# Spectral weights copied by ScalarE into mode-wise rows, mixed sums stored by GpSimd, part of the weights loaded among images

## The reference, cut to what matters

```python
def spectral_conv2d(x, w1, w2):                       # MODES = 16
    x_ft = jnp.fft.rfft2(x)
    out_ft = out_ft.at[:, :, :MODES, :MODES].set(jnp.einsum('bixy,ioxy->boxy', x_ft[:, :, :MODES, :MODES], w1))
    out_ft = out_ft.at[:, :, -MODES:, :MODES].set(jnp.einsum('bixy,ioxy->boxy', x_ft[:, :, -MODES:, :MODES], w2))
    return jnp.fft.irfft2(out_ft, s=(h, w))
...
x1 = spectral_conv2d(x, w1, w2)                       # x: group-normed input, 16 x 64 x 128 x 128, fp32
x2 = jnp.einsum('bchw,oc->bohw', x, conv_w) + conv_b[None, :, None, None]
y_flat = (x1 + x2).transpose(0, 2, 3, 1).reshape(-1, c)
y_flat = kan_linear(y_flat, k1_base, k1_spline, k1_scaler, grid)   # silu and cubic splines, 64 x 64
y_flat = kan_linear(y_flat, k2_base, k2_spline, k2_scaler, grid)
return x + gelu(y)
```

## Time and profile before

| | us |
|---|---|
| median of 3 runs | 3696.25 |
| lowest and highest | 3695.16, 3698.87 |
| the profiled execution | 3700.55 |
| its span | 3698.7 |
| TensorE busy in it | 3629.4 (98%) |
| VectorE, ScalarE busy | 3480.8, 3374.5 |
| barrier to mix block | 248.72 |
| first inverse matmul of the second half | 334.23 |

### The profile page before, as it was taken

The page is one execution under the profiler, slowest core; times in us unless marked ns, Lnnn a source line. Parts: engine busy times, 40 slices in busy tenths (PEclk is TensorE's granted clock), DMA queues, the critical chain, the costliest instruction groups (busy, mean ns, idle before and its releaser), DMA issues.

```text
span 3698.7 us, 98607 instructions
## 1 busy us (share of the span) xinstructions
PE 3629.4 (98%) x36932; PEld 1565.2 (42%) x36932; DVE 3480.8 (94%) x3548; ACT 3374.5 (91%) x3510; POOL 116.3 (3%) x140
## 2 busy tenths in 40 slices
PE   8987999999999999999999999999999999999998
PEld 4555657654333333333333333333333333333333
DVE  8875999999999999999999999999999999999997
ACT  4433999999999999999999999999999999999997
POOL 0000000000000000000000000000000000000000
PEclk9998999999999999999999999999999999999999
DMA  9998243432322323223232232322323222232231
GB/s 320 328 214 200 61 120 89 118 93 60 76 69 65 77 58 76 68 66 77 58 76 67 67 74 60 77 66 68 73 61 77 64 70 71 63 77 64 70 73 50
DMA packets 269760, 338.45 MB, mean 92 GB/s; under 512 B 83272, under 2 KB 198824, under 8 KB 267624
## 3 DMA queue, kind: packets, MB, share of 16 engines
q1 hardware_dynamic: 248392, 265.50, 25.3%
q0 software_dynamic: 18720, 67.49, 10.1%
q10 hardware_dynamic: 2560, 4.20, 0.4%
HBM read 248.50 MB, written 88.61 MB: 91 GB/s over the span
## 4 chain that ended last, share of the span: by engine, by line
PE 90%; SPq 1%; issue 1%; DMA 1%; ACTq 0%; ACT 0%; DVE 0%; DVEq 0%
PE l_ps L1241 84%; PE y_banks L1218 3%; PE y_banks L1227 2%; SPq L160 1%; PE y_banks L1260 1%; PE y_banks L1202 1%; PE y_banks L1189 0%; PE y_banks L1241 0%; DMA big<-in_spec_w_i_dram 0%; ACTq L729 0%; ACT mixed L726 0%; DMA rows_scratch<-rows 0%; PE l_ps L1260 0%; DMA modes_scratch<-mixed 0%; PE mix_ps L705 0%
## 5 line engine op out<-in xcount | busy, mean ns | idle before, releaser
L1121 ACT ACTIVATE offset<-size 128x1024 f32<-128x1024 f32 x1280 | 1241.0, 1045 | 8.1
L1047 DVE SCALAR_TENSOR_TENSOR cube0r<-below,offset 128x1024 f32<-128x1024 f32 x256 | 312.6, 1221 | 113.2 <-ACT offset L1121 103.2
L1047 DVE SCALAR_TENSOR_TENSOR cube2r<-below,offset 128x1024 f32<-128x1024 f32 x256 | 311.5, 1217 | 0.6 <-PE l_ps L1241 0.6
L1047 DVE SCALAR_TENSOR_TENSOR cube0l<-above,offset 128x1024 f32<-128x1024 f32 x256 | 311.7, 1217 | 0.0
L1047 DVE SCALAR_TENSOR_TENSOR cube1r<-below,offset 128x1024 f32<-128x1024 f32 x256 | 311.6, 1217 | 0.0
L1047 DVE SCALAR_TENSOR_TENSOR cube1l<-above,offset 128x1024 f32<-128x1024 f32 x256 | 311.6, 1217 | 0.0
L1047 DVE SCALAR_TENSOR_TENSOR cube3r<-below,offset 128x1024 f32<-128x1024 f32 x256 | 311.5, 1217 | 0.0
L1047 DVE SCALAR_TENSOR_TENSOR cube2l<-above,offset 128x1024 f32<-128x1024 f32 x256 | 311.5, 1217 | 0.0
L1047 DVE SCALAR_TENSOR_TENSOR cube3l<-above,offset 128x1024 f32<-128x1024 f32 x256 | 311.5, 1217 | 0.0
L1047 DVE SCALAR_TENSOR_TENSOR cube4l<-above,offset 128x1024 f32<-128x1024 f32 x256 | 311.4, 1217 | 0.0
L1047 DVE SCALAR_TENSOR_TENSOR cube4r<-below,offset 128x1024 f32<-128x1024 f32 x256 | 311.4, 1216 | 0.0
(11 more groups left out here) (169 smaller groups left out, 5963.3 us busy)
## 6 DMA issues: line engine op xcount, KB each, us to landing
big<-in_x_dram SPq DMA_DIRECT2D x128, 512.0 KB, 8.3
x_ring<-in_x_dram SPq DMA_DIRECT2D x256, 256.0 KB, 4.6
out_dram<-act_out SPq DMA_DIRECT2D x128, 512.0 KB, 2.6
act_out<-in_x_dram POOLq DMA_DIRECT2D x127, 512.0 KB, 7.0
rows_t<-rows_scratch SPq DMA_DIRECT2D x512, 32.0 KB
rows_scratch<-rows SPq DMA_DIRECT2D x14, 1024.0 KB, 6.8
pair_t<-pair_scratch SPq DMA_DIRECT2D x128, 65.0 KB, 1.9
big<-in_spec_w_r_dram SPq DMA_DIRECT2D x16, 512.0 KB, 11.6
```

The costliest lines, as they stand in the source:

```text
L1047: nc.vector.scalar_tensor_tensor(out=cube[q][side][:], in0=distance[own][:], scalar=EDGE - KNOTS[q], in1=offset[own][q][:], op0=ALU.min, o ...
L1121: nc.scalar.activation(offset[own][q][:], size[own][:], ACT.Square, bias=-KNOTS[q]).then_inc(offset_ready[layer], 1)
```

## The change

- **The copy.** ScalarE copies the weights of each unit, 64 channels x 16 modes, from `mix_w` into one of two buffers `relaid`, in which the 64 channels of a mode lie in a row (`relay`, L758 of the changed kernel). TensorE takes its moving operand from there. The second buffer lies in spare room of `stats`. ScalarE waits for the weights' landing now, and TensorE for `relaid_ready`. In ScalarE's program the copy of a unit stands ahead of the evacuation of the unit before it.
- **The stores.** GpSimd's queue issues the 32 stores of the sums, ScalarE none.
- **Weights among images.** 56 of the 64 output channels of w1's real part are loaded behind images 2 to 15, four channels at a time, in two DMAs of 128 KB; 8 channels are left to be loaded behind the last image. The 20 loads behind the barrier are as before.
- **The chain ahead of unit 0.** The means and the bias of the pairs stand behind the first units (VectorE and TensorE); the table of Sqrt is loaded at the end of the forward block, by a root that nobody uses.
- **The start.** TensorE waits for the table `dft_h_sb` and the image, and for the two other tables only ahead of the first turn. The eight small arrays of the splines are loaded by ScalarE's queue.

```diff
@@ -149,16 +150,29 @@
...
+O_IMAGE = 4
+O_AMONG = O_IMAGE * (B - 2)
...
+def load_mix_weights_among(sp, t, dst, image):
+    for half in range(2):
+        x0 = SH * half
+        sp.dma_start(dst[half * C:(half + 1) * C, bass.ds((image - 2) * O_IMAGE, O_IMAGE), :, :],
+                     t["w1_r"][:, bass.ds((image - 2) * O_IMAGE, O_IMAGE), x0:x0 + SH, :]).then_inc(t["mix_loaded"][0][0], 16)
...
@@ -362,7 +377,7 @@
...
-            sp.dma_start(dft_h_sb[:], t["dft_h"]).then_inc(tables_loaded, 16)
+            sp.dma_start(dft_h_sb[:], t["dft_h"]).then_inc(dft_h_loaded, 16)
...
@@ -395,22 +410,13 @@
...
                     next_image(b2, par)
+                    sp.wait_ge(weights_turned, len(TURNS))
+                    load_mix_weights_among(sp, t, weights[:, 2], 2 * b2 + par)
...
-            sp.wait_ge(weights_turned, len(TURNS))
-            load_mix_weights(sp, t, weights[:, 2], 0, 0, 0, C)
+            load_mix_weights(sp, t, weights[:, 2], 0, 0, O_AMONG, C)
             load_mix_weights(sp, t, weights[:, 3], 0, 1, 0, C // 2)
...
-        @block.gpsimd
-        def _(pool):
-            for l, (b_, s_, c_) in enumerate(((t["k1_base"], t["k1_spline"], t["k1_scaler"]),
-                                              (t["k2_base"], t["k2_spline"], t["k2_scaler"]))):
-                own = slice(l * C, (l + 1) * C)
-                pool.dma_start(kan["spline"][own], s_).then_inc(natural_loaded, 16)
...
@@ -520,6 +526,8 @@
...
+                    if k == 1 and not before:
+                        pe.wait_ge(tables_loaded, 32)
...
@@ -549,7 +557,7 @@
...
-            pe.wait_ge(tables_loaded, 48)
+            pe.wait_ge(dft_h_loaded, 16)
...
@@ -594,6 +602,13 @@
...
+                nc.scalar.dma_start(kan["spline"][own], s_).then_inc(natural_loaded, 16)
+                nc.scalar.dma_start(kan["scaler"][own], c_).then_inc(natural_loaded, 16)
+                nc.scalar.dma_start(kan["mats"][own, F_SILU, :], b_).then_inc(natural_loaded, 16)
+                nc.scalar.dma_start(kan["mats"][own, NF, :], t["conv_w"]).then_inc(natural_loaded, 16)
...
@@ -605,6 +620,8 @@
...
+            act.wait_ge(averages_set, 2)
+            nc.scalar.activation(root_of_one, avg[:, 0:1], ACT.Sqrt)
...
@@ -654,6 +671,8 @@
...
+        relaid = [sb("relaid0", [P, MODES, C])[:], spare[:, 2 * NRM:2 * NRM + MODES * C].rearrange("p (k o) -> p k o", o=C)]
+        relaid_ready = sem("relaid_ready")
...
@@ -678,33 +697,47 @@
...
+            for n in range(2 * SH):
+                u = n % KEPT
+                pool.wait_ge(mix_kept, n + 1)
+                for col in range(2):
+                    pool.dma_start(modes_dram[n, :, :, :, col, :].rearrange("r h b f -> (r h b) f"),
+                                   mixed[u][col * C:(col + 1) * C, :]).then_inc(stored[u], 16)
...
-                    pe.wait_ge(t["mix_loaded"][g][part], 32 * (C // MIX_O))
...
+                        pe.wait_ge(relaid_ready, 2 * SH * g + SH * part + x + 1)
+                        own_w = relaid[x % RELAID]
                         if g == 1 and part == 0:
                             pe.wait_ge(mix_kept, x + 1)
+                        if g == 0 and part == 0 and x == 2:
+                            bias()
+                        if g == 0 and part == 0 and x == SH - 2:
+                            pe.wait_ge(bias_kept, 1)
...
-                                    normed[u][:, ky, :, :, :].rearrange("p f h b -> p (f h b)"), mix_w[g][part][:, :, x, ky],
+                                    normed[u][:, ky, :, :, :].rearrange("p f h b -> p (f h b)"), own_w[:, ky, :],
...
@@ -715,21 +748,29 @@
...
-                    act.wait_ge(mix_done, 2 * SH * g + SH + x + 3)
-                    if n >= KEPT:
-                        act.wait_ge(stored[u], 32 * (n // KEPT))
-                    nc.scalar.activation(mixed[u][:], ps[x][:], ACT.Copy).then_inc(mix_kept, 1)
-                    act.wait_ge(mix_kept, n + 1)
-                    for col in range(2):
-                        nc.scalar.dma_start(modes_dram[n, :, :, :, col, :].rearrange("r h b f -> (r h b) f"),
...
+            def relay(unit):
+                g, part, x = unit // (2 * SH), unit // SH % 2, unit % SH
+                if x == 0:
+                    act.wait_ge(t["mix_loaded"][g][part], 32 * (C // MIX_O if g + part else B - 1))
+                if unit >= RELAID:
+                    act.wait_ge(mix_done, unit - RELAID + 3)
+                nc.scalar.activation(relaid[unit % RELAID].rearrange("p k o -> p o k"), mix_w[g][part][:, :, x, :],
+                                     ACT.Copy).then_inc(relaid_ready, 1)
+            def evacuate(unit):
+                g, x = unit // (2 * SH), unit % SH
+                n = SH * g + x
+                act.wait_ge(mix_done, unit + 3)
+                if n >= KEPT:
+                    act.wait_ge(stored[n % KEPT], 32 * (n // KEPT))
+                nc.scalar.activation(mixed[n % KEPT][:], ps[x][:], ACT.Copy).then_inc(mix_kept, 1)
+            for unit in range(4 * SH):
+                relay(unit)
+                if unit and (unit - 1) // SH % 2 == 1:
+                    evacuate(unit - 1)
+            evacuate(4 * SH - 1)
...
@@ -752,18 +793,23 @@
...
-            for half in range(2):
-                rows = slice(half * C, (half + 1) * C)
-                link(nc.vector.tensor_copy(pair_mean[rows, :], mean_c[rows, half:B:2]))
-                link(nc.vector.tensor_tensor(pair_rm[rows, :], rs_c[rows, half:B:2], pair_mean[rows, :], ALU.mult))
-            dve.sem_inc(rm_ready, 1)
...
+            def means_of_pairs():
+                for half in range(2):
...
+            def bias_of_pairs():
+                dve.wait_ge(bias_done, 1)
...
@@ -772,24 +818,32 @@
...
+            for x2 in range(SH // 2):
+                for u in range(2):
+                    norm(0, 0, x2, u)
+                if x2 == 0:
+                    means_of_pairs()
+                if x2 == 1:
+                    bias_of_pairs()
...
```

91 lines of the change are left out of this document (47 added, 44 removed).

## The result

The changed kernel takes 3708.73 us in the median (3706.04 to 3711.37, 7 runs), the kernel before 3695.6 us beside it (3693.02 to 3699.38, 7 runs). The ratio is 1.0032, with a 95% interval of 1.0023 to 1.0041: slower by 13 us, where I had forecast +3.5 and put the upper end at 3707.0. The profiled execution of the changed kernel is its fastest, 3706.04 us with a span of 3704.0.

What follows compares the result with a forecast made beforehand. TensorE's spline products in the second half bound the kernel unchanged, so only their start shifts: -0.8 (start) + 3.2 (copy) + 1.1 (store) = +3.5 us, a median of 3699.8 us, range 3690.5 to 3707.

Steps and rivals of the forecast that it cites:

- Weights among images: nothing on the path: Forward part: 14 images' pairs of weight loads fit beside TensorE's 13.70 us an image, costing 0.
- rival C: Forward part: loads among images cost over 1.9 us an image, so x comes late; 3706 us, chance 0.06.
- the pair's 1.37 us: Forward part: DMA time an image for two 128 KB weight loads, each a quarter of a 512 KB load's 2.73 us.
- My margin, 0.28 us an image: Forward part: slack between TensorE's 13.70 us an image and the DMAs' 13.42, besides loading already saved up.
- The start, -0.8: Kernel start: TensorE starts without waiting for unneeded tables, so image 1 begins at most 0.8 us earlier.
- The shorter chain, 0: Behind the barrier: unit 0 starts some 3 us earlier, but later units wait for weights, so 0 gained.
- The last landing 63.3 us behind the barrier: Mix stage: the same 20 DMAs of 512 KB follow the barrier, so the last weights still land 63.3 us later.
- rival D: Mix weights: those moved among images do shorten the path, by 19.6 us, to 3680 us; chance 0.03.
- The copy, 1.93 us, +3.2: Mix units: ScalarE's scattered copy takes 1.93 us and sets the pace, adding 3.2 us after the last landing.
- rivals A and B: ScalarE's copy: A, not slowed by its stride, 3693.2 us, chance 0.20; B, 2.75 us a copy, 3712 us, chance 0.09.
- The store, +1.1: End of the mix stage: the last stores on GpSimd's queue issue and land 1.1 us later, ends 0.1 to 2.8.

Runs made afterwards that it cites:

- e13: The changed kernel with the two 128 KB loads after each image each landing in all 128 partitions instead of 64, weights wrongly ordered; ratio 1.0011, +6.0 us.
- e4: The changed kernel with the loads of the first real part issued by GpSimd in place of SP; ratio 1.0014, +5.8 us.
- e3_again: One more execution of e3, nothing changed; 3704.0 us.
- e3: The changed kernel with ScalarE's copy written in a row, so TensorE multiplies wrongly ordered weights; ratio 1.0024, +11 us.
- e1: The changed kernel without loads among images, all of the first real part loaded behind the last image; ratio 1.0009, +4.0 us.
- e9: The changed kernel with four one-channel loads over all 128 partitions after each image, in place of two four-channel loads over 64; ratio 1.0189, +69 us.
- e7: The changed kernel without loads among images and without ScalarE's copy, leaving the start, shorter chain and GpSimd's stores; ratio 1.0006, +2.5 us.
- e8: As e7, but ScalarE issues the stores, leaving only the start and the shorter chain; ratio 0.9996, -1.1 us.
- e10: The kernel before, with the ten loads behind the barrier that land in partitions 64 to 127 issued by GpSimd beside SP's ten; ratio 1.0003.
- e15: As e7, but ScalarE issues the stores of the last two units and GpSimd those of the first 14; ratio 1.0001.

## Why the prediction was wrong

**The step that failed is "Weights among images: nothing on the path", "I take 0".** The forward part lost 7.6 us; rival C, at 0.06, is what happened, at a price over the 1.9 us an image that it asked for. The term that was mis-sized is the pair's 1.37 us. From image 3 to image 15 the changed kernel needs 14.20 us an image (56.16 to 226.53 over twelve), so the pair costs 14.20 - 12.05 = 2.15 us. (In its second profile the waiting sets in later, and the pitch from image 6 on is 14.31.) The slices show the same: thirteen of 0.34 us at 239 in place of 348 are 1.4 us missing, and the 0.26 MB of the pair are 0.75 us at the full rate. I had scaled the issue pace of a 512 KB load of weights, between its like; beside x the narrow load slows the wide ones too (e13), and on a queue of its own it stays within the slack (e4). My margin, 0.28 us an image, was thinner than any such error. I said that rows 4 spoke against C; a row of one kind of load alone cannot say what a mixture costs.

**The start, -0.8: not shown.** Image 1 began 0.6 and 1.0 us earlier in the two profiles of the changed kernel. But of the 14 profiles of kernels with this start, image 1 stood at 28.5 to 28.8 in 6 and at 29.7 to 30.4 in 8; their mean is 29.49, and that of the 5 profiles with the old start (29.2 to 29.6) is 29.48. The early ones have the path of the forecast: in e3_again TensorE turns the kernel's weights at 24.02, released by VectorE's chain. Two executions of the same kernel, e3, show both. Its second group of sixteen matmuls is what differs, e3 first, then e3_again:

```profile
11.88 3.69 PE L497 MATMUL along_h<-big,dft_h_sb 64*64 64x512 f32 x16 [0.65 <-issue]
...
30.15 2.38 PE L497 MATMUL along_h<-big,dft_h_sb 64*64 64x512 f32 x20 [1.16 <-ACT turned_w L617]
```

```profile
11.88 1.95 PE L497 MATMUL along_h<-big,dft_h_sb 64*64 64x512 f32 x16 [0.82 <-DMA big<-in_x_dram]
...
28.68 3.66 PE L497 MATMUL along_h<-big,dft_h_sb 64*64 64x512 f32 x32 [1.11 <-ACT turned_w L617]
```

TensorE starts earlier, but the time at which its matmuls go from 3.69 to 1.95 us a group, their pace in the rest of the forward part, doesn't follow it in each execution. What decides it is open. The granted clock doesn't tell the two apart; from 12 to 15.5 us it is shown as 1.00 for both, first the one with 16 matmuls done, then the one with 32:

```profile
12.00:15.50 3.50, 3.50 (x16) 0.74 (x16) 3.40 (x4) 0.37 (x1) 0.00 (x0) 1.00 1.09 349
```

```profile
12.00:15.50 3.50, 3.46 (x32) 1.70 (x35) 3.32 (x4) 1.25 (x5) 0.00 (x0) 1.00 1.09 347
```

A gain of 0.8 that hangs on this is no gain to count on; that both profiles of the changed kernel are of the early ones is luck.

**The shorter chain, 0: right.** The first unit is 3.9 us behind the barrier in place of 7.2 (251.70 in e1, forecast 252), and nothing of it shows at the end.

**The last landing 63.3 us behind the barrier: right within 1.6 us**, and rival D is dead. The 1.5 us that it gave back are not the change's: in all profiles with these same twenty loads behind the barrier it lies between 60.6 (e9) and 64.1 (e7), in e1, without loads among images, at 61.4, and in the second pair at 62.8 before and 62.4 changed.

**The copy, 1.93 us, +3.2: right.** 1.98 to 2.00 and +3.1. Rows 6, VectorE's scattered write, was the right row to take, and rivals A and B fell. The rule of one element a cycle, which I had put beside it from the Trainium skill's "ScalarE: Activation LUTs" ("What ACT_TABLE_LOAD costs"), does not hold for this write; for the plain one of e3 it fits as before. That the units of the middle would gain nothing was right too: unit 24 waits 7.80 us for its weights.

**The store, +1.1: too small, and its mechanism wrong in the main.** The block ends 2.9 us later, just over my upper end of 2.8; TensorE's first inverse matmul, which I had reckoned to, comes 1.8 later. I looked for all of it in issue and landing, which cost 0.6 in e7 against e8. The larger part, 2.1 us there, lies in the end of the block, which I had not costed at all.

**The sum.** With 7.6 in place of 0, 1.5 given back behind the barrier and 2.9 in place of 1.1, -0.6 + 7.6 - 1.5 + 3.1 + 2.9 = +11.5 us at the start of the second half. The second pair of profiles divides nearly the same total otherwise: -1.0 + 6.8 - 0.4 + 3.5 + 3.0 = +11.9. Here e8's -1.1, e1's +4.0 and the changed kernel's +13.1 in the medians fit the terms within 2 us. My forecast against the median had used a profiled execution that held a stop of some 5 us of its own; that did not hurt the forecast, since I worked with differences, but it made the first comparison of the two profiles look like half the loss.

## What to carry to other kernels

A load that fits into the DMAs' idle share by its own duration may still not fit: ask in how many partitions it lands and what stands behind it in the queue, and give the slack that is left a size before relying on it. If such a load must go among wide ones, spread it over all partitions; on a queue of its own it cost less here too. And when the last DMA of a block moves to another engine, the engine's way to the end of the block moves with it: look at what the next block's first instruction waits for, not only at the landing.

## What the runs showed of the hardware

- Loads of 128 KB into 64 partitions, in line with loads into 128, pull the rate of both down: 239 GB/s over 4.5 us for 0.26 MB of weights, against 317 to 342 if the same bytes land in 128 partitions.
- Behind the barrier, weights alone, 260 to 265 us: 188 GB/s in 512-byte runs into 64 partitions at a time, 209 with the halves of the partitions on two queues, 224 in 8 KB runs into 64.
- Two queues with weight loads of the same shape: GpSimd's moved 5.78 MB (0.5 of it a store) in packets of 3.6 KB while SP's moved 2.27 MB in packets of 0.5 KB (e10, 250 to 290 us).
- Loads whose slowest dimension in DRAM has two steps moved 38 GB/s (e9).
- ScalarE's ACTIVATE of 1024 fp32 elements: 1.05 us written in a row, 1.98 to 2.00 with each element 256 bytes from the last.
- With the last stores on GpSimd's queue a block ended 2.6 us behind SP's last load of what they stored, with the last ones on ScalarE's 0.5 us (e7, e8, e15).
- The second half holds stops of TensorE, "issue" in the chain, that come in one execution and not in the next of the same kernel: 2.91 us at 774.80, then 0.44.
